# Normed tiles 2 and 3 of the first batch turned by transposing transfers, and one shared block in other banks

## The reference

```python
# layer 1: "attention" is a plain product with the fake-quantised context
x = x + tanh(g_xattn) * (fake_quant(layernorm(x)) @ fake_quant(ctx))      # per batch, ctx is 1024 x 1024
# layer 2: a mixture of 16 experts (2 per token) beside a shared block
xt = layernorm(x).reshape(-1, 1024)
gate = top2(softmax(xt @ router_w + router_b) + router_bias)
y = sum_e gate[:, e] * ((silu(xt @ ew1[e] + eb1[e]) * (xt @ ew2[e] + eb2[e])) @ ew3[e] + eb3[e])
z = (silu(xt @ sw1 + sb1) * (xt @ sw2 + sb2)) @ sw3 + sb3                 # shared, width 512
x = x + tanh(g_ffn) * (y + z)
```

## Time and profile before

| what | us |
|---|---|
| median of 3 runs | 317.61 (316.82 to 317.87) |
| the profiled execution, its own time | 318.93 |
| the profiled execution, span from first to last instruction | 317.0 |
| TensorE busy in the span | 294.3 |
| VectorE busy | 222.6 |
| ScalarE busy | 115.1 |

### The profile page before, as it was taken

One profiled execution on the slowest core, in us unless ns is written; L12 is line 12 of the kernel. 1 busy time (PEld: TensorE's weight loads), 2 busy tenths in 40 slices (PEclk: granted clock), 3 DMA queues, 4 the chain that ended last, 5 costly groups with the idle time before them and its releaser, 6 DMA issues.

```text
span 317.0 us, 4650 instructions
## 1 busy us (share of the span) xinstructions
PE 294.3 (93%) x1868; PEld 149.5 (47%) x1868; DVE 222.6 (70%) x392; ACT 115.1 (36%) x130; POOL 25.3 (8%) x34
## 2 busy tenths in 40 slices
PE   0398998989999999999999999999999999999993
PEld 0234598954444444644444444444444444444441
DVE  2898987895698863686465988877794859759210
ACT  1898558759562450200352404402006040100000
POOL 2010201000001310000000021101101110000000
PEclk9999999999999999999999999999999999999997
DMA  7999260249940555000698420000000000500302
GB/s 280 413 323 319 69 196 7 83 144 219 340 149 0 96 104 132 2 2 0 189 316 292 173 95 2 0 0 0 2 0 0 2 1 0 237 31 1 132 33 103
DMA packets 34164, 35.56 MB, mean 112 GB/s; under 512 B 16068, under 2 KB 28380, under 8 KB 34012
## 3 DMA queue, kind: packets, MB, share of 16 engines
q1 hardware_dynamic: 34128, 35.23, 35.7%
q10 hardware_dynamic: 12, 0.00, 0.0%
HBM read 27.88 MB, written 4.20 MB: 101 GB/s over the span
## 4 chain that ended last, share of the span: by engine, by line
PE 80%; DVE 11%; ACT 3%; DMA 2%; issue 1%; POOL 1%; ACTq 0%; DVEq 0%
PE PS L1526 26%; PE PS L1367 20%; PE PS L1559 11%; PE PS L1552 7%; PE PS L1402 7%; PE PS L1314 4%; DVE stats L771 3%; DMA sc<-in_g_ffn_dram 2%; PE PS L1321 1%; DVE X L837 1%; PE PS L1383 1%; DVE S2f L807 1%; DVE areaW L820 1%; POOL lnR L471 1%; DVE wrow L846 1%
## 5 line engine op out<-in xcount | busy, mean ns | idle before, releaser
L1367 PE MATMUL PS<-areaT,areaW 128*128 128x512 f16 x288 | 62.6, 379 | 1.1 <-DVE SA L851 1.1
L1367 PEld LDWEIGHTS PS<-areaT,areaW 128*128 128x128 f16 x288 | 27.9, 98 | 34.6 <-DVE SA L851 1.3
L1526 PE MATMUL PS<-areaT,area 128*128 128x512 f16 x192 | 42.1, 379 | 0.0
L1526 PE MATMUL PS<-areaT,areaW 128*128 128x512 f16 x192 | 42.1, 379 | 0.0
L1314 PE MATMUL PS<-area,areaQ 128*128 128x512 f16 x128 | 32.2, 402 | 1.8 <-DVE area L803 1.1
L1035 DVE SCALAR_TENSOR_TENSOR X<-PS,cf,X 128x512 f32<-128x512 f32 x22 | 15.5, 745 | 20.0 <-PE PS L1559 15.2
L1526 PEld LDWEIGHTS PS<-areaT,areaW 128*128 128x128 f16 x192 | 18.8, 98 | 22.6
L1526 PEld LDWEIGHTS PS<-areaT,area 128*128 128x128 f16 x192 | 18.8, 98 | 22.6
L771 DVE BATCH_NORM_STATS2 stats<-X 128x6 f32<-128x512 f32 x32 | 20.5, 684 | 4.3 <-DMA X<-in_x_dram 4.1
L1552 PE MATMUL PS<-SW,areaH 128*128 128x512 f16 x96 | 21.9, 379 | 0.0
L1314 PEld LDWEIGHTS PS<-area,areaQ 128*128 128x128 f16 x128 | 12.7, 103 | 18.1 <-issue 3.6
(11 more groups left out here) (187 smaller groups left out, 411.9 us busy)
## 6 DMA issues: line engine op xcount, KB each, us to landing
ring<-in_L_ffn_sw_dram SPq DMA_DIRECT2D x12, 512.0 KB, 5.1
X<-in_x_dram SPq DMA_DIRECT2D x8, 512.0 KB, 7.4
areaT<-in_ctx_dram SPq DMA_DIRECT2D x8, 512.0 KB, 8.6
ring<-in_ctx_dram SPq DMA_DIRECT2D x8, 512.0 KB, 4.0
ring<-in_L_ffn_ew_dram SPq DMA_DIRECT2D x16, 256.0 KB, 5.5
out_dram<-X SPq DMA_DIRECT2D x7, 512.0 KB, 2.7
ring<-in_L_ffn_ew_dram SPq DMA_DIRECT2D x2, 1024.0 KB, 4.9
areaQ<-gate_dram SPq DMA_DIRECT2D x1, 1024.0 KB, 6.4
```

What stands on the lines that cost most here:

```text
L1367: last = mm(PS[:, SU_BANK[half * SC + c] + w, lo:hi], SW[:, wp, 2 * c + w, k, :], XT[:, xp, k, tk], start=(k == 0 and n == 0), stop=(k == ...
L1526: last = mm(PS[:, EU_BANK[u] + w, :], W12S[j][:, wp, k, cs], XT[:, xp, k, b * S:(b + 1) * S], start=(k == 0 and n == 0), stop=(k == KC - 1 ...
```

## The change

Tiles 2 and 3 are no longer turned by TensorE. SyncE issues `turn_tokens(2)` and `turn_tokens(3)` for them, between the loads of the shared weights and the first loads of the second batch's context, with two new semaphores `xt0_in`. TensorE waits for these before `first_blocks(2)` and `first_blocks(3)`, and ScalarE's four copies out of banks 0 and 1 are gone. Block 2 of the shared up projection is summed in banks 0 and 1, so its wait for `su_gate(0)` is gone. The waits of the second batch's products follow the new banks. On VectorE, `ln2_lo(2)` stands ahead of `bn(3)`.

```diff
-        SU_BANK = (4, 6, 4, 6, 4, 2, 6, 4)
+        SU_BANK = (4, 6, 0, 4, 4, 2, 6, 4)
...
+        xt0_in = [sem("xt0_in0"), sem("xt0_in1")]
...
+                signal = xt_in[i - TB] if i >= TB else xt0_in[i - 2]
                 sp.dma_start_transpose(XT[:, :, :, i * P:(i + 1) * P].rearrange("p h k t -> p (h k) t"), WROW[i])\
-                    .then_inc(xt_in[i - TB], 16)
-
-            for r in range(4, 12):
+                    .then_inc(signal, 16)
+
+            for r in range(4, 8):
+                load_chunk(r)
+            turn_tokens(2)
+            turn_tokens(3)
+            for r in range(8, 12):
                 load_chunk(r)
...
             for i in range(TB):
                 ln_rows(i)
-                tk_hi_evac(i)
-                tk_lo_evac(i)
+                if i < 2:
+                    tk_hi_evac(i)
+                    tk_lo_evac(i)
...
             attend(3)
+            ln2_lo(2)
             bn(3)
-            ln2_lo(2)
...
-                if half == 0 or c == 3:
-                    pe.wait_ge(su_hf, half * SC + (c - 1 if half == 0 else 1))
+                if c == 3:
+                    pe.wait_ge(su_hf, half * SC + 1)
...
-                if i < TB - 1:
-                    transpose_tokens(i + 1)
+                if i == 0:
+                    transpose_tokens(1)
...
             for i in range(TB):
-                pe.wait_ge(tk_hi, i + 1)
-                pe.wait_ge(tk_lo, i + 1)
+                if i < 2:
+                    pe.wait_ge(tk_hi, i + 1)
+                    pe.wait_ge(tk_lo, i + 1)
+                else:
+                    pe.wait_ge(xt0_in[i - 2], 16)
                 first_blocks(i)
...
                 if i == TB:
-                    pe.wait_ge(tk_hi, TB)
-                    pe.wait_ge(tk_lo, TB)
+                    pe.wait_ge(su_hf, SC - 1)
                 if i == TB + 1:
                     pe.wait_ge(r1_rdy, B)
-                if i >= TB + 2:
-                    pe.wait_ge(su_hf, i - TB + 1)
+                if i == TB + 2:
+                    pe.wait_ge(su_hf, SC)
```

More of the change, by code:

```diff
@@ L549, in ln_rows @@
                 if i in (TB, TB + 1):
-                    act.wait_ge(tk_T, 2 * TB)
+                    act.wait_ge(tk_T, 4)
                 if i >= TB + 2:
@@ L633, in _ @@
             quant_ctx(1, 7)
-            act.wait_ge(tk_T, 2 * TB)
+            for j in range(2):
+                act.wait_ge(xt0_in[j], 16)
             su_silu_of(3)
```

## The result

The changed kernel takes 319.95 us (median of 9 runs, 318.56 to 321.36) and the kernel before 316.82 us in the 9 runs measured beside it, the three shown above among them. The ratio is 1.0073, with a 95% interval of 1.0047 to 1.0098: slower by about 2.3 us, 1.5 to 3.1. The time lies 0.8 us above the forecast, but the two were not added to the same base: the forecast put 1.54 us on 317.61, the median of 3 runs, and the 9 runs of the kernel before have 316.82. Between the medians of the 9 runs lie 3.1 us, by the ratio 2.3. The profiled execution of the changed kernel took 319.29 us, with a span of 317.6, against 318.93 and 317.0 before.

The account below looks back on a forecast made before the run. TensorE was busy 294.3 of 317.0 us, but the second batch's quantising chain through `su_gate(0)` set 88.83. Tile 3 1.96 us late, less 0.42 absorbed, gave +1.54: 317.61 + 1.54 = 319.15, forecast 319.2, range 318.2 to 321.0.

Parts of the forecast that it names:

- Tile 2: TensorE before `first_blocks(2)`: transfer issued at 51.00, landing in 4.4 us, start at 55.45 after a wait of 3.8 us.
- Tile 3, the working without the clock: TensorE before `first_blocks(3)`: transfer issued at 57.44, landed at 61.84, start at 61.89 instead of 59.93, 1.96 us later.
- GpSimd's power, the term with two ends: In tile 3's statistics: taken as 0.55 us, ending at 53.20; the other end, 1.48 us, would add 0.93.
- The forecast takes nothing: TensorE behind tile 2's wait: no time added for a slow clock, though bounded between nothing and 4.6 us.
- Rival A: Clock falls in tile 2's wait, TensorE restarts slow: 0.6 to 2.1 us on top of 1.54, say 320.3; chance 0.30.
- the slack ahead of tile 3: Tile 2 ends 0.92 us ahead of tile 3's landing, which swallows a slow stretch of 1.8 us.
- The argument against A: The clock's fall about 2.2 us after work stopped was seen in one instance only, at the program's very end.
- the 1.04 us of the earlier trace: At the start, 8 transposes behind a wait took 1.04 us against 0.61 later; read as the slow clock.
- I carry the 1.54 whole to the products: From `su_gate(0)`, 1.54 us later, through the context to the second batch's products: nothing absorbed, 88.83 becomes 90.37.
- The bank wait worth nothing: Ahead of block 2: removing its wait is worth up to 1.1 us to TensorE and nothing to the time.
- the 0.61 us named "issue": TensorE's wait at 88.83 ahead of the second batch's products: really for `s2_rdy`, VectorE's last context sum ending at 88.73.
- The wait ahead of the products: TensorE ahead of the second batch's first products: wait grows from 0.61 to about 1.4 us, products at 90.4.

Follow-up runs that it names:

- the transfers alone: The changed kernel with block 2's old banks and the old waits for `su_hf` put back; 320.72 us, ratio 1.0074 to the kernel before.
- the kernel with the fetch moved: The changed kernel plus 9 wide and 66 single-column unread matmuls in TensorE's wait for tile 2; 322.15 us, ratio 1.0124 to the kernel before.
- the kernels with the 15 matmuls: The changed kernel plus 15 unread matmuls in tile 2's wait, 322.05 us; also with context loads held until tile 3 landed, 322.15 us.

## Why the prediction was right, and where its steps were off

The sign, the place and about the size were right: 319.2 forecast, 319.95 measured, within the range. But it is a sum in which one term was missing and another too large, and that these two came out alike is luck. So is part of the nearness of the times, since the base of the forecast was 0.8 us above the median of the 9 runs; the step itself was 2.3 us against 1.54.

*Tile 2* was right to a few hundredths once the execution's offset of 0.35 us is taken off: issue 51.00 became 50.68, the landing took 4.4, the wait 3.81, the start 55.45 became 55.10.

*Tile 3, the working without the clock* was right. GpSimd's power, the term with two ends, took the 0.55 us that I chose for it:

```profile
52.29 0.55 POOL L477 TENSOR_TENSOR lnR<-lnV,mhalf 128x1 f32<-128x1 f32 x1 [5.81 <-DVE lnV L782]
```

and with the clock kept up the tile started at 15.69 behind 0.86 us of wait, where the forecast has 61.89 - 46.12 = 15.77 and 0.9.

*"The forecast takes nothing" for the clock failed.* Rival A happened: in the profiles of the change, its repetition and every kernel that kept both transfers and left the wait unfilled, tile 2's 64 matmuls took 5.37 us or more. Of the 1.6 us lost there the slack ahead of tile 3, 0.92 by the forecast, swallowed 1.0, so A came at its low end: 0.6 us. In the profile of the transfers alone it was 1.5, within A's 0.6 to 2.1. The mean granted clock of the executions says that a fall is the rule: at most 0.994 in 12 of the 15 of the change and in none of the 63 of the kernel before that were timed beside the experiments (its profiled one has 0.995, with the fall behind its last matmul). The argument against A, that there was one instance only and at the very end, was weak: a wait longer than the 2.2 us after which a fall had been seen should have been given the better chance. The prediction also read the 1.04 us of the earlier trace rows as the slow clock; the windows view has a granted clock of 1.00 for 14 to 15 us of that trace, so that row doesn't show it.
The Trainium skill ("TensorE: Matmul & The Clock Gate", section "HAM oscillation — how this bites in real kernels") says that waits for transfers between short groups of matmuls let the next group start at the slow clock. This case's traces agree, with 5.37 against 3.73 us behind the wait of 3.81 and 6.03 against 3.61 behind one of 3.18.

*"I carry the 1.54 whole to the products" failed too, in the other direction.* `su_gate(0)` moved by 2.08 us and the products by 1.29; in the repetition by 2.04 and 1.71. Up to the issue of chunk 13's load the chain was as stiff as the forecast took it: 13.2 us from `su_gate(0)` to that issue before, 13.1 in the change and its repetition. From that chunk's use to the products it was 5.7 and 5.6. What was lost went mostly at the landing: the load was issued at 80.56 instead of 78.91, 1.65 later, and used at 84.20 instead of 83.12, 1.08 later; ScalarE's wait for it went from 3.27 to 2.62 us. In the repetition it was used 4.09 us after its issue, before 4.21. Why it landed sooner in the first profile stays open. The DMA engines were no idler while this load was under way (a share of 1.03 from 78.91 to 83.09 before, 1.09 from 80.56 to 84.17 in the change), and over all the profiles but that with the late chunk the landing scatters between 3.6 and 4.6 us, with no order between the kernels. So it was a transfer among others and not a fixed delay, and part of what was lost can be the chance of one execution. Over the two profiles of each kernel `su_gate(0)` moved by 2.07 and the products by 1.6, so about +0.5 and -0.5 cancelled; the mean shift of the last matmuls is (265.33 + 265.74 - 264.03 - 263.85) / 2 = 1.6 us against the 1.54 forecast.

*The bank wait worth nothing* was right, and shown from both sides (1.0013 alone, 1.0074 for the transfers without it). So was the reading that the 0.61 us named "issue" was the context's chain: easing that chain made the kernel faster by 0.3% and the wait vanished. The wait ahead of the products grew to 0.65 and 1.11 us in the two profiles and not to 1.4, since the slow clock held TensorE back as well.

*What stays open.* The measured 2.3 us (1.5 to 3.1) are 0.7 more than the 1.6 of the profiles. The profiled executions of the change (spans 317.6 and 318.4) lie below the middle of its 15 spans (318.5), those of before (317.0, 316.7) above the middle of the 63 (316.2), so part of it is which executions were profiled. What the longer executions lose is not seen in any profile of the change. Two other profiles show what it could be. In the transfers alone the clock fell sooner and tile 3 started 0.85 us later, in an execution with a mean granted clock of 0.985, the value of the change's longest execution (span 319.7) as well. In the kernel with the fetch moved it was a late chunk 13 and a second fall of the clock ahead of the products. That is argued, not shown.

## What to carry to other kernels

Before work is moved from a busy engine to a transfer, price the wait that replaces it: its length, the slow clock after it, and who is served from the late end; 16 transposes of tile 2 and a wait of 1.1 us, 2.15 us together (49.69 to 51.84 before), were traded for 3.8 us of waiting and 1.6 of slow clock. A wait taken away from the busiest engine is worth something only if no second chain ends at the next meeting point: the bank and the sooner low half brought nothing measurable alone, and about 1.2 us once the context's chain was shortened. And where the profile says "issue" for a short wait, look for the last writer of the awaited signal before believing it.

## What the runs showed of the hardware

The fetching of instructions takes part in the traffic of the DMA engines, as packets of 16 KB in a queue of its own, each of which held one engine for 0.9 us or more (the one shown above 0.94). All eight late landings of a tile's transposing transfer (5.2 to 6.1 us instead of 4.2 to 4.4) had such a packet between issue and landing; eight other transfers had one as well and landed in 4.2 to 4.6. So the packet goes with every late landing, but it doesn't always make one. With 15 instructions added on TensorE tile 3's transfer had the packet in it and was late; with 60 more ahead of the place the packet had moved and the landing was back at 4.4. So adding a few instructions on TensorE can make a distant transfer late.

The clock fell in, or up to 1.3 us behind, idle stretches of 3.2 to 3.8 us between dense work, and TensorE then worked at 1.2 GHz for some 3.4 to 5.3 us, at a cost of 1.6 to 2.5 us each time (5.37 and 6.25 against 3.73, 6.03 against 3.61). Behind the waits of 2.5 and 2.6 us for tile 3 in the kernels with the 15 matmuls it stayed up.
